# The last layer of a fused model on one core: second matrix as rows of features with transposes, router rows between rank tiles

## What is computed

```python
weights = (einsum('bsd,do->bso', x, wr) + br)[..., 0]      # the router's weight of each token
_, idx = top_k(weights, k)                                  # k = half of S; the best k - 1 are kept
h = gelu(einsum('bkd,dh->bkh', x[idx], w1) + b1)            # 64 -> 256 features
y = einsum('bkh,hd->bkd', h, w2) + b2                       # 256 -> 64 features
out = x;  out[idx] += y * weights[idx]
```

## Time and profile before

| | us |
|---|---|
| median of 3 runs (1071.45 to 1074.3) | 1072.88 |
| the profiled execution | 1069.42 |
| its span, first to last instruction | 1067.3 |
| of it, the tail: first router row to the end | 993.40 to 1067.3 |

### The profile page before, as it was taken

The page is one execution under the profiler, slowest core; times in us unless marked ns, Lnnn a source line. Parts: engine busy times, 40 slices in busy tenths (PEclk is TensorE's granted clock), DMA queues, the critical chain, the costliest instruction groups (busy, mean ns, idle before and its releaser), DMA issues.

```text
span 1067.3 us, 11533 instructions
## 1 busy us (share of the span) xinstructions
PE 835.7 (78%) x3813; PEld 356.5 (33%) x3813; DVE 800.2 (75%) x1054; ACT 512.5 (48%) x1015; POOL 542.3 (51%) x356
## 2 busy tenths in 40 slices
PE   7873665767865997976887878878888878879887
PEld 4441334646733333431121111111111111115465
DVE  1248998865532444389999999999999999984475
ACT  1365300185252775664555555555554444434621
POOL 0010749420010000016999999999999999880100
PEclk9987855687565999995667685665556576659987
DMA  9100000700100000011011011011011011000001
GB/s 389 41 0 1 0 0 20 154 1 1 60 1 0 2 2 0 1 29 35 22 43 27 17 43 38 8 40 40 9 38 43 10 34 43 1 0 1 1 16 28
DMA packets 20505, 33.09 MB, mean 31 GB/s; under 512 B 10078, under 2 KB 19294, under 8 KB 19422
## 3 DMA queue, kind: packets, MB, share of 16 engines
q1 hardware_dynamic: 20446, 32.36, 10.7%
HBM read 17.57 MB, written 1.20 MB: 18 GB/s over the span
## 4 chain that ended last, share of the span: by engine, by line
PE 40%; DVE 32%; issue 12%; ACT 9%; POOL 4%; SPq 1%; DMA 1%; DVEq 0%; ACTq 0%; POOLq 0%
DVE pair_arrays L1618 14%; DVE pair_arrays L1602 5%; PE PS L574 4%; PE PS L749 4%; PE PS L721 3%; PE PS L420 3%; PE PS L731 3%; PE PS L510 2%; PE PS L841 2%; ACT PS L896 2%; ACT token_weights L896 2%; PE PS L481 2%; DVE pair_arrays L1424 2%; PE PS L867 2%; ACT pair_arrays L896 2%
## 5 line engine op out<-in xcount | busy, mean ns | idle before, releaser
L1258 POOL TENSOR_TENSOR pair_arrays<-pair_arrays 128x736 f32<-128x736 f32 x192 | 332.4, 1743 | 25.7 <-DVE pair_arrays L1618 25.1
L896 ACT ACTIVATE PS<-PS,A_negative 128x368 f32<-128x368 f32 x384 | 191.3, 538 | 130.1 <-PE PS L731 129.5
L1618 DVE TENSOR_TENSOR_SCAN pair_arrays<-PS,scan_carry,pair_arrays 128x368 f32<-128x368 f32 x256 | 237.1, 972 | 0.4
L1602 DVE TENSOR_TENSOR pair_arrays<-pair_arrays,PS 128x736 f32<-128x736 f32 x144 | 129.7, 901 | 8.4 <-PE PS L721 8.3
L749 PE MATMUL PS<-pair_arrays,weights 128*32 128x368 f32 x768 | 134.1, 730 | 1.2 <-POOL pair_arrays L1258 1.1
L1212 POOL TENSOR_TENSOR big<-pair_arrays 128x1104 f32<-128x1104 f32 (+15 forms) x32 | 55.9, 1766 | 131.1 <-DVE pair_arrays L1375 68.5
L1618 DVE TENSOR_TENSOR_SCAN pair_arrays<-PS,pair_arrays 128x368 f32<-128x368 f32 x128 | 110.6, 909 | 2.7 <-ACT PS L896 2.7
L721 PE MATMUL PS<-spread_rows,token_weights 96*128 96x368 bf16 x192 | 68.5, 452 | 37.8 <-DVE pair_arrays L1602 24.1
L1266 POOL TENSOR_TENSOR pair_arrays<-pair_arrays,token_weights 128x736 f32<-128x736 f32 x48 | 83.9, 1747 | 18.4 <-DVE big L1580 18.4
L721 PE MATMUL PS<-pair_arrays,token_weights 96*128 96x368 bf16 x192 | 67.2, 445 | 25.9 <-DVE pair_arrays L1602 20.1
L481 PE MATMUL PS<-big,weights 128*128 128x368 f32 (+15 forms) x192 | 62.7, 493 | 31.3 <-DVE big L1435 20.1
(11 more groups left out here) (190 smaller groups left out, 1244.1 us busy)
## 6 DMA issues: line engine op xcount, KB each, us to landing
big<-in_x SPq DMA_DIRECT2D x4, 2048.0 KB, 17.3
big<-decay_rows SPq DMA_DIRECT2D x4, 1104.0 KB, 16.3
spread_rows<-pair_arrays SPq DMA_DIRECT2D x96, 46.0 KB, 1.9
pair_arrays<-pair_arrays SPq DMA_DIRECT2D x96, 46.0 KB, 1.9
spread_rows<-big SPq DMA_DIRECT2D x48, 46.0 KB, 1.9
pair_arrays<-big SPq DMA_DIRECT2D x48, 46.0 KB, 1.9
weights<-in_wts SPq DMA_DIRECT2D x1, 2204.0 KB, 18.0
big<-in_wexp SPq DMA_DIRECT2D x1, 1536.0 KB, 7.8
```

The costliest lines, as they stand in the source:

```text
L896: return nc.scalar.activation(o, i, fn, **kw)
L1258: nc.gpsimd.tensor_tensor(hcbuf[t % NRING], hbuf[t % NRING], c4(seg).unsqueeze(1).to_broadcast([128, 2, G]), ALU.mult).then_inc(s("hc_read ...
L1602: tt(bx[t % NRING], b4(seg).unsqueeze(1).to_broadcast([128, 2, G]), PS[:, 2:4, 0:G], ALU.mult).then_inc(s("b_used"), 1)
L1618: nc.vector.tensor_tensor_scan(hbuf[t % NRING][:, h, :], PS[:, 4 + 2 * (t % 2) + h, 0:G], bx[t % NRING][:, h, :], carry[:, a:a + 1] if k e ...
```

## The change

Five things, all in the tail.

1. The second matrix has features as rows: `outputs(p, k)` takes `w2` as the loaded weights (64 columns) and `hid` as the moving data (368 columns). The two batches of a pair go to partitions 0 to 63 and 64 to 127 of one PSUM bank (bank 7, the only one it uses); four matmuls for each pair and group. ACT adds `b2` while it copies to `ffn`. `output_rows(p, i)` then transposes both batches of a pair at once, in three pieces of 4, 4 and 1 token tiles.
2. `rows_of` has two operations instead of three, and goes by batch and piece: 256, 256 and 64 columns.
3. Ahead of the loop stand the router rows of the first two batches and the columns of the first. The rows of the third and fourth batch stand behind the first three rank tiles, the other columns behind the third, fourth and fifth. The hidden of the first batch moves behind tiles four to nine.
4. The residual rows move to the second batch, the second matrix of a pair behind tiles of its second batch (`between`), its transposes to the third batch and to the last three tiles of the fourth. The hidden of the fourth batch goes in twos behind the first three tiles.
5. Twelve transfers out instead of nine; the packed weights lose 64 columns (`b2row`) and gain one.

```diff
-            weight_rows(0)
-            for b in range(1, B):
-                weight_rows(b)
-                weight_columns(b - 1)
-            weight_columns(B - 1)
+            for m in range(NG + 1):
+                weight_row(m)
+            weight_columns(0)
+            for m in range(NG + 1, 2 * NG):
+                weight_row(m)
+
+            def between(b, j):
+
+                if b == 0 and j < NG:
+                    weight_row(2 * NG + 2 * j)
+                    weight_row(2 * NG + 2 * j + 1)
+                if b == 0 and j >= NG:
+                    hidden(b, j - NG)
+                if b == 0 and NG - 1 <= j < NG + 2:
+                    weight_columns(j - 1)
+                if b in (1, 2) and j < 2 * NG:
+                    hidden(b, j)
+                if b == 1 and j < len(RESID):
+                    residual_rows(j)
+                if b == 1 and j >= 2 * NG:
+                    outputs(0, j - 2 * NG)
+                if b == 2 and j in (1, 3, 5):
+                    output_rows(0, j // 2)
+                if b == 3 and j < NG:
+                    hidden(b, 2 * j)
+                    hidden(b, 2 * j + 1)
+                if b == 3 and NG <= j < 2 * NG:
+                    outputs(1, j - NG)
+                if b == 3 and j >= 2 * NG:
+                    output_rows(1, j - 2 * NG)
...
-            def rows_out(x_):
-
-                n, members = ROWS[x_]
...
-                for i, (b, j) in enumerate(members):
-                    t0 = j * 128
-                    for hh in range(2):
-                        last = nc.tensor.matmul(PS[0:n, 2 * ((x_ + 1) % 2), i * D:(i + 1) * D], hid[b][:, hh, t0:t0 + n],
-                                                w("w2")[:, hh * D:(hh + 1) * D], start=(hh == 0), stop=(hh == 1))
+            def outputs(p, k):
+
+                pe.wait_ge(s("hid_ready"), (2 * p + 1) * 2 * NG + NG + k + 1)
+                if p or k:
+                    pe.wait_ge(s("ffn_ev"), p * NG + k)
+                for hh in range(2):
+                    for b2 in range(2):
+                        last = nc.tensor.matmul(PS[half(b2), 7, 0:G], w("w2")[:, hh * D:(hh + 1) * D], hid[2 * p + b2][:, hh, cols(k)],
+                                                start=(hh == 0), stop=(hh == 1), skip_group_check=True)
+                last.then_inc(s("ffn_ps"), 1)
+
+            def output_rows(p, i):
+
+                j0, nj, n = TILES[i]
+                pe.wait_ge(s("ffn_ev"), NG * (p + 1))
...
+                for j in range(nj):
+                    last = nc.tensor.transpose(PS[0:n, i, j * 128:(j + 1) * 128], ffn[:, p, (j0 + j) * 128:(j0 + j) * 128 + n], w("ident"))
...
+                if b % 2:
+                    for k in range(NG):
+                        act.wait_ge(s("ffn_ps"), b // 2 * NG + k + 1)
+                        f(ffn[:, b // 2, cols(k)], PS[:, 7, 0:G], ACT.Identity, bias=col("b2")).then_inc(s("ffn_ev"), 1)
...
-                step(tt(y, PS[0:n, 2 * ((x_ + 1) % 2), 0:4 * D].rearrange("q (i d) -> q i d", i=4),
-                        w("b2row")[0:n, :].unsqueeze(1).to_broadcast([n, 4, D]), ALU.add))
-                dve.wait_ge(s("sel_ready"), members[-1][0] + 1)
-                step(tt(y, y, weight.unsqueeze(2).to_broadcast([n, 4, D]), ALU.mult))
+                dve.wait_ge(s("sel_ready"), b + 1)
+                step(tt(y, PS[0:n, i, 0:nj * 128].rearrange("q (j b d) -> q j b d", j=nj, b=2)[:, :, b % 2, :],
+                        sel3[0:n, b, j0:j0 + nj].unsqueeze(2).to_broadcast([n, nj, D]), ALU.mult))
```

More of the change, by code:

```diff
@@ L815, in weight_columns @@
                 last.then_inc(s("wcol_ps"), 1)
-            weight_rows(0)
-            for b in range(1, B):
-                weight_rows(b)
-                weight_columns(b - 1)
-            weight_columns(B - 1)
-            def fill(b):
-                steps = [[] for _ in range(NT)]
-                for y in range(2 * NG):
-                    steps[y].append((hidden, (b, y)))
-                if b == 0:
-                    for i in range(len(RESID)):
-                        steps[i + 1].append((residual_rows, (i,)))
-                else:
-                    steps[1].append((rows_out, (2 * (b - 1),)))
-                    steps[4].append((rows_out, (2 * (b - 1) + 1,)))
-                return steps
+            for m in range(NG + 1):
[26 more added lines that the diff above has]
+                    output_rows(1, j - 2 * NG)
             def hidden(b, y):
@@ L874, in _ @@
                     pe.wait_ge(s("sel_ready"), b - 1)
-                steps = fill(b)
                 for j in range(NT):
@@ L884, in _ @@
                     last.then_inc(s("rank_ps"), 1)
-                    for work, args in steps[j]:
-                        work(*args)
-            for x_ in range(2 * (B - 1), len(ROWS)):
-                rows_out(x_)
+                    between(b, j)
         @block.scalar
@@ L1161, in weight_columns, with weight_row @@
                 f(wcol[0:LAST, b, NT - 1:NT], PS[0:LAST, 2, b * NT + NT - 1:b * NT + NT], ACT.Copy).then_inc(s("wcol_ev"), 1)
-            for b in range(B):
-                for k in range(NG):
-                    m = b * NG + k
-                    act.wait_ge(s("wrow_ps"), m + 1)
-                    f(wrow[b][:, cols(k)], PS[:, m % 2, 0:G], ACT.Identity, bias=col("br")).then_inc(s("wrow_ev"), 1)
-                if b:
-                    weight_columns(b - 1)
-            weight_columns(B - 1)
+            def weight_row(m):
+                act.wait_ge(s("wrow_ps"), m + 1)
+                f(wrow[m // NG][:, cols(m % NG)], PS[:, m % 2, 0:G], ACT.Identity, bias=col("br")).then_inc(s("wrow_ev"), 1)
+            for m in range(NG + 1):
+                weight_row(m)
+            weight_columns(0)
+            for m in range(NG + 1, B * NG):
+                weight_row(m)
+            weight_columns(1)
             def residual_part(i):
@@ L1704, in _ @@
                         select(b - 1)
-                    if b and j == 4:
-                        rows_of(2 * (b - 1))
-                    if b and j == 7:
-                        rows_of(2 * (b - 1) + 1)
+                    if b == 2 and j >= 2 * NG:
+                        rows_of(0, j - 2 * NG)
+                    if b == 3 and 2 <= j < 5:
+                        rows_of(1, j - 2)
+            for i in range(len(TILES)):
+                rows_of(2, i)
             select(B - 1)
-            for x_ in range(2 * (B - 1), len(ROWS)):
-                rows_of(x_)
+            for i in range(len(TILES)):
+                rows_of(3, i)
 def pack(inputs):
```

74 lines of the change are left out of this document (32 added, 42 removed).

## The result

The changed kernel took 1056.49 us (median of 4 runs, 1054.1 to 1061.84) against 1072.16 for the kernel before (4 runs), a ratio of 0.9858 with a 95% interval of 0.9814 to 0.9902. Two more sets of runs gave 1059.79 (6 runs; ratio 0.9877, 0.9851 to 0.9903) and 1059.51 (4 runs; 0.9878, 0.9861 to 0.9895). It is faster, by 12 to 16 us; the prediction was 1060.3, a gain of 12.6.

A forecast was written before the change was run, and what follows sets the result against it. DVE and PE take turns in the second batch; PE bounds the last two, its clock being low. Terms -3.3 + 1.45 - 7.2 - 3.55 = -12.6 us: 1069.42 becomes 1056.8, median 3.46 above, 1060.3; range 1056.5 to 1068.5.

The forecast's parts named there:

- The sum: Whole tail: -3.3 (head) + 1.45 (second batch) - 7.2 (third) - 3.55 (fourth and end) = -12.6 us.
- signs of being wrong: `outputs` near 2.5; clock 0.50 in last two batches; fourth batch's first count behind 1037; a stage ahead of 993 that moved.
- Head: Tail's start to the second batch's first rank count: count at 1012.65 instead of 1015.96, 3.3 us gained.
- The halves side by side: Second matrix: four half-width matmuls run side by side in 1.24 us, against 2.48 one after another.
- the 7.4 of the rival: Rival, halves go one after another: six `outputs` cost 1.24 more each, 7.4 us, so 1067.7; chance 0.11.
- Second batch: Second batch's first count to the third's: PE the bound, 12.8 us, with two waits for ACT's copy of 0.75 each.
- Third batch: Third batch's first count to the fourth's: DVE the bound, 8.5 us at full clock, 7.2 gained.
- The two rivals of a low clock through whole batches: Low clock in third and fourth batch, 1074.6, chance 0.09; or already from the second batch, 1085, chance 0.03.
- Fourth batch: Fourth batch's first count to the end of PE's transposes: PE the bound at full clock, 11.8 us.
- a short fall of the clock: Rival ahead of the fourth batch: about four of six hidden at 1.2 GHz, 2.8 us less gain, 1063.1; chance 0.27.
- the gap at 1014 to 1016 before: Kernel before: PE also had a gap there and the clock stayed at 1.00, held against the short fall.
- End: Behind the last transposes: DVE's chain 5.8 us, to 1051.55, then 3.17 to the end of the span, 1054.7.

The follow-up runs named there:

- e_bank0: Changed kernel with only the first pair's second `outputs` group (second batch) in another PSUM bank, bank 3; tail 60.28 us.
- e_bank: Changed kernel with the second `outputs` group of both pairs in another PSUM bank, bank 3; tail 58.5 us, median of a repeat 1056.34 us.

## Why the prediction was right, step by step

**The sum.** The tail was to be 61.3 us and was 62.0. The difference of 0.7 is made of the stages in the table: -0.5, +0.4, -0.1, +1.9, -0.5, -0.5. That it is so small is in part luck: 2.3 us too much in two stages met 1.6 too little in the others. The median of 1060.3 lies beside 1056.49, 1059.79 and 1059.51. The first is at the lower end of the range (1056.5), and not for the reason given there: the tail gained 11.9 of the 15.7, less than forecast, and the rest lies elsewhere, as far as the traces show in the stretch ahead of the tail, which the prediction did not forecast. Two of its signs of being wrong are in the first trace, a start of the fourth batch behind 1037 (1038.33) and a stage ahead of 993 that moved. Both are that stretch: from the first router row it is 40.35 us to the fourth batch, where 40.55 was forecast.

**Head.** Right: 18.74 for 19.25, and DVE's first `beats` 5.49 us behind the first router row, where the prediction had 5.6 (999 against 993.4). The experiment with the old head lost 4.6 to 4.7, of which up to 2.0 is a lower clock. Alone in the kernel before it gained nothing, which the sum of separate terms did not show.

**The halves side by side.** Right, and the term on which most hung: 1.39 us for a group where 1.24 was taken, two instructions at a time in the trace, and 7.1 us more at full width, for the 7.4 of the rival.

**Second batch.** 13.23 for 12.8. The mechanism was right, the size of two terms small: 1.39 for 1.24 for a group, 0.83 (2.22 less 1.39) for 0.75 for a wait. Taking the waits away gave 1.38 for the 1.5 predicted.

**Third batch.** 8.38 for 8.5, with the clock at 1.00 and DVE as the bound. The two rivals of a low clock through whole batches did not come. One of them had a rule of the Trainium skill behind it, "TensorE: Matmul & The Clock Gate", Part 4, that transposes do not count as busy in the same way: with nine of them among six hidden matmuls the row of the third batch shows 1.00, so none of that is seen here.

**Fourth batch.** Here the forecast failed, with 13.72 for 11.8 to DVE's end chain: it took the clock to be full, and the rival "a short fall of the clock" came true, at the place it named. Its size was half of what was put: two matmuls' worth of hidden went at 1.2 GHz, not four (2.80 and 1.70 for two pairs that take 1.50), 1.43 by the experiments against 2.8. What spoke against it, the gap at 1014 to 1016 before, was no evidence: behind the same instructions the clock fell at a gap in e_bank0 and stayed in e_bank. The rest of the 1.9 is the groups and waits, as in the second batch. By the prediction's own rival the time would have been 1063.1; shorter stages elsewhere and the smaller fall made up for it.

**End.** DVE's chain took 5.27 for 5.8. An operation of 256 columns that follows another on the same data starts 0.46 later as forecast (1052.05 to 1052.51), but the next piece's only 0.34 after that, and the small piece costs 0.25 and 0.14. From DVE's last operation to the end it was 2.41 to 2.81 in the traces of this study with the changed end, 3.17 before. The last transfer is a quarter of the size; that this is the reason, no run tests.

## What to carry to other kernels

Two matmuls that each fill half the columns of TensorE cost here little more than one of full width (1.39 us for a group, half of 2.54), so for a matrix with 64 output features it can pay to load it as weights for two batches at once, with the transposes that this costs. A gain at the head of a chain is worth what the later stages do with it: look at the clock there before counting it. Where groups share one PSUM bank through a copy, a second bank for every other one took 2.5 us of waits out of this tail. Filling the gap on PE ahead of long matmuls took 1.4 out where the clock would have fallen, and nothing where it stayed. Compare two such kernels stage by stage, and look at the clock of both before putting a difference down to the edit.

## What was not expected of the hardware

The order in which the four half-width matmuls are written makes no difference (1.39 us for a group either way, two instructions at a time). The clock can fall behind a gap of 1.8 us on PE in one run and not in another, with the same instructions up to it. With the same instructions, too, the tail began up to 6.9 us earlier or later, and its head then took 18.7 or 19.3 us.
